# Layer 0 of a four-layer graph kernel: units sized by the spread of destinations, row sums and count copies on ScalarE, dense blocks loaded from its queue

## The reference, cut to what matters

```python
# x (6250, 256); src, dst (100000,), dst sorted and denser at low numbers; edge_weight (100000,)
edge_index = jnp.stack([src, dst])
x = _layernorm(x + L0(x, src, dst, edge_weight, L0_gnn_W), axis=-1)      # the layer that is changed
x = _layernorm(x + L1(x, edge_index, ...), axis=-1)
x = _layernorm(x + L2(x, src, dst, edge_weight, ...), axis=-1)
x = _layernorm(x + L3(x, edge_index, ...), axis=-1)

def L0(x, edge_row, edge_col, edge_val, W):
    msgs = edge_val[:, None] * x[edge_col]
    agg = jax.ops.segment_sum(msgs, edge_row, num_segments=6250)
    return agg @ W.T
```

## Time and profile before

| | |
|---|---|
| time before, median of 3 runs | 4154.18 us (4149.27 to 4157.17) |
| the profiled execution's own time | 4150.73 us |
| its span | 4149.5 us |
| granted TensorE clock, mean | 0.869 |
| DVE busy over the span | 2069.3 us (50%) |
| ACT busy | 1087.8 us (26%) |
| PE busy | 3049.1 us (73%) |
| POOL busy | 2525.4 us (61%) |
| comparison of group 0 (line 995) starts at | 69.7 us |
| last indirect transfer of layer 0's pass starts at | 1491.4 us |

### The profile page before, as it was taken

How to read it: one execution, slowest core, us unless ns; L and a number is a source line. 1 busy time by engine, 2 the same in 40 slices (tenths; PEclk the granted TensorE clock), 3 DMA queues, 4 the chain that set the end, 5 groups by cost and what they waited for, 6 DMA issues and landing times.

```text
span 4149.5 us, 56706 instructions
## 1 busy us (share of the span) xinstructions
PE 3049.1 (73%) x17920; PEld 2113.4 (51%) x17920; DVE 2069.3 (50%) x7275; ACT 1087.8 (26%) x2612; POOL 2525.4 (61%) x2372
## 2 busy tenths in 40 slices
PE   3887777777767637779957996777667675798975
PEld 2665555455555525534434554565555543555543
DVE  7998788886666526432233224432322345222249
ACT  1344444454545525500040002400000035000016
POOL 3767666665555444267736771177777744777755
PEclk9999898998989868789967998888888887899985
DMA  6666666777666647478825673554444334877743
GB/s 242 80 120 92 126 129 127 141 144 144 141 140 136 155 87 222 148 193 240 235 82 155 196 200 84 165 158 135 138 135 136 114 104 168 274 217 220 215 123 107
DMA packets 485739, 639.73 MB, mean 154 GB/s; under 512 B 79146, under 2 KB 427524, under 8 KB 480708
## 3 DMA queue, kind: packets, MB, share of 16 engines
q0 software_dynamic: 153600, 258.41, 30.6%
q1 hardware_dynamic: 331844, 377.70, 28.9%
HBM read 427.79 MB, written 208.12 MB: 153 GB/s over the span
## 4 chain that ended last, share of the span: by engine, by line
PE 24%; POOL 24%; DVE 20%; issue 14%; DMA 10%; ACT 4%; DVEq 2%; SPq 1%; POOLq 0%; ACTq 0%
POOL rows_buf L723 23%; PE PSA L754 6%; DVE accT L1169 5%; PE PSA L528 4%; DMA T<-S 3%; PE PSA L772 3%; DMA accT<-Awd 3%; DVE rows_buf L1003 2%; PE PSA L1137 2%; DMA rows_buf<-T,idx 2%; PE PSA L1038 2%; DVE accT L1177 2%; PE PSA L1219 2%; DVE big L1123 2%; DVE stat L536 1%
## 5 line engine op out<-in xcount | busy, mean ns | idle before, releaser
L1292 POOL DMA_INDIRECT A<-rows_buf,big x572 | 896.2, 1567 | 532.1 <-ACT rows_buf L1064 252.7
L723 POOL DMA_INDIRECT rows_buf<-T,idx x888 | 841.3, 947 | 293.7 <-issue 273.3
L772 PE MATMUL PSA<-S,rows_buf 128*128 128x128 bf16 (+2 forms) x5904 | 593.0, 262 | 359.7 <-DMA rows_buf<-X,idx 204.0
L772 PEld LDWEIGHTS PSA<-S,rows_buf 128*128 128x128 bf16 (+2 forms) x5904 | 553.0, 151 | 436.4 <-issue 343.7
L823 DVE TENSOR_TENSOR accT<-PSA,accT 128x256 f32 (+2 forms) x354 | 132.8, 375 | 1212.9 <-PE PSA L772 1204.2
L723 POOL DMA_INDIRECT rows_buf<-X,idx x528 | 502.4, 952 | 312.0 <-issue 309.5
L1169 DVE TENSOR_TENSOR accT<-PSA,accT 128x784 f32 (+1 forms) x444 | 360.1, 811 | 229.0 <-PE PSA L1137 160.1
L1137 PE MATMUL PSA<-big 128*128 128x272 bf16 (+2 forms) x796 | 229.4, 362 | 231.5 <-DVE accT L1169 230.3
L1054 PE MATMUL PSA<-XRS,rows_buf 128*128 128x256 f32 x1144 | 312.5, 397 | 2.1 <-ACT rows_buf L1064 2.1
L1137 PEld LDWEIGHTS PSA<-big 128*128 128x128 bf16 x796 | 76.5, 121 | 336.8 <-DVE accT L1169 320.1
L754 PE MATMUL PSA<-XRS,rows_buf 128*64 128x512 bf16 (+3 forms) x912 | 242.9, 380 | 0.0
(11 more groups left out here) (273 smaller groups left out, 5650.0 us busy)
## 6 DMA issues: line engine op xcount, KB each, us to landing
XRS<-Ad SPq DMA_DIRECT2D x144, 512.0 KB
Ad<-accT SPq DMA_DIRECT2D x28, 1568.0 KB, 6.7
rows_buf<-Ad SPq DMA_DIRECT2D x72, 512.0 KB
XRS<-in_xpad SPq DMA_DIRECT2D x192, 128.0 KB, 3.9
rows_buf<-A SPq DMA_DIRECT2D x48, 512.0 KB, 4.5
A<-accT SPq DMA_DIRECT2D x3, 6272.0 KB
Awd<-accT SPq DMA_DIRECT2D x6, 3136.0 KB, 9.9
X<-rows_buf SPq DMA_DIRECT2D x144, 128.0 KB, 1.9
```

The lines of the kernel that those rows point to most:

```text
L723: s_hg[i % RING].on(pool.indirect_dma_start(Gv(i % RING, j), None, table, bass.IndirectOffsetOnAxis(idx[:, c:c + 1], 0)), 16)
L772: last = pe.matmul(PS[i % 2][0:F, W * h:W * h + W], Gv(i % RING, j)[:, o:o + F], hits[:, i % SRING, j, :], start=j + part == 0, stop=j == ...
L1292: pool.indirect_dma_start(A, bass.IndirectOffsetOnAxis(tgt[:, c:c + 1], 0), G[:, i % RING, j, :], None, compute_op=ALU.add).then_inc(s_k[n ...
```

## The change

1. **Unit sizes.** Seven classes (CLASSES) replace four: chunks 0 to 63 in fours with 8 slots, 64 to 119 in pairs with 8, 120 to 159 in pairs with 10, 160 to 251 single with 8, 252 to 375 in pairs with 20, 376 to 447 single with 14, the rest single with 16. Units go from 444 to 366, hot ones from 192 to 156; those of windows 6 to 11 from 84 to 52, those of windows 12 to 27 from 168 to 158. The one-hot ring OHRING goes from 8 to 6, and the planner's cost is another one.
2. **Duplicates.** PE adds a third product in source_rows: 16384 is added wherever the other edge comes later, so that Eq holds only equal and not later ones. For groups below BYACT (92) the row sums of Eq are then taken by ACT (row_sums, four ACTIVATEs), DVE waits for them and compares with 1. From group 92 on DVE sums as before. targets stands at another place in DVE's order: for groups up to 92 behind the first unit_out of its own group.
3. **Late counts.** In the windows behind the hot ones (12 to 27), every second unit (83 in all: 9 of 980 columns, 36 of 686, 38 of 784) is copied from PSUM to SBUF as bf16 by ACT (unit_copy); PE's next unit waits for that copy, and DVE adds from the copy.
4. **Dense blocks.** SP issues only the loads of blocks 0 and 1; block t + 2 is issued on ACT's queue behind dense_turned(t).
5. **Waits.** In onehots, waits on units that DVE has itself added already are left out; others are for one unit later than before.

```diff
+MAXN = 20
+UC = NT * MAXN
-OHRING = 8
+OHRING = 6
...
+CLASSES = ((0, 64, 4, 8), (64, 120, 2, 8), (120, 160, 2, 10), (160, HOTW, 1, 8),
+           (HOTW, 376, 2, MAXN), (376, 448, 1, 14), (448, HOT, 1, 16))
...
+    u.copied = TURN[u.w] > LASTHOT and u.at % 2 == 1
...
-    cost = lambda u: 1.2 * u.k + 0.4
+    cost = lambda u: 1.2 + 0.7 * u.k if u.hot else 0.2 + 0.051 * u.n + u.k * (0.35 + 0.0128 * u.n)
...
-            for t in range(NT):
-                if dense_step(t) + 1 == p:
-                    dense_load(t)
+                for t in range(2):
+                    dense_load(sp, t)
...
-                pe.matmul(o, srch[:, c:c + 1].broadcast_to([128, 128]), identb[:, :], start=True, stop=False)
+                pe.matmul(o, lowerb[:, :], identb[:, :], start=True, stop=False)
+                pe.matmul(o, srch[:, c:c + 1].broadcast_to([128, 128]), identb[:, :], start=False, stop=False)
...
+        def row_sums(i):
+
+            if i < BYACT:
+                sc.wait_ge(s_eq, i + 1)
+                for j in range(CG):
+                    last = sc.activation(junkA[:, j, :], Eq[:, i % 2, j, :], ACT.Identity, accum_out=cnt[:, G0 + i, j:j + 1])
+                last.then_inc(s_rs, 1)
+
         def targets(i):
...
+            if i < BYACT:
+                v.wait_ge(s_rs, i + 1)
+                least = 1.0
...
+        def built(q):
+
+            if q.at >= spread.evicted:
+                v.wait_ge(s_am, q.at + 1)
+                if q.hot:
+                    v.wait_ge(s_amw, q.hots + 1)
...
+                before = UNITS[u.at - 1]
+                if before.copied:
+                    s_ca.of(pe, ("unit", before.at))
+                else:
+                    pe.wait_ge(s_ae, u.at)
...
+                s_ca.mark(("unit", u.at), sc.activation(ABW[:, 0:NT * u.n], AB[:, 0:NT * u.n], ACT.Identity))
...
+            if u.copied:
+                s_ca.of(v, ("unit", u.at))
+                got = ABW[:, 0:NT * u.n]
...
                     dense_turn(t)
                     dense_turned(t)
+                    if t + 2 < NT:
+                        dense_load(sc, t + 2)
+            if i + 1 < NCOLD:
+                row_sums(i + 1)
```

More of the change, by code:

```diff
@@ L78, in natural_units @@
     us = []
[L79 removed]
+    for lo, hi, k, n in CLASSES:
         for c in range(lo, hi, k):
@@ L98 @@
 TURN = {w: i for i, w in enumerate(ORDER)}
+for u in UNITS:
+    u.copied = TURN[u.w] > LASTHOT and u.at % 2 == 1
+for u in UNITS:
+    u.copies = sum(q.copied for q in UNITS[:u.at])
 def unit_at(p):
@@ L355, in build @@
     pool.tensor_copy(identb[:, :], ident[:, :])
+    pool.tensor_scalar(lowerb[:, :], lower[:, :], float(FAR), None, ALU.mult)
     pool.memset(ones[:, :], 1.0)
@@ L411, in build @@
     u = 0
-    for lo, hi, k, n in ((0, PAIR, 2, NS), (PAIR, HOTW, 1, NS), (HOTW, TWO, 2, US), (TWO, HOT, 1, US)):
+    for lo, hi, k, n in CLASSES:
         m = (hi - lo) // k
@@ L996, in equals @@
                             srcf[:, g, :].unsqueeze(2).broadcast_to([128, CG, 128]), ALU.is_equal).then_inc(s_eq, 1)
+        def row_sums(i):
[4 more added lines that the diff above has]
+                last.then_inc(s_rs, 1)
         def targets(i):
             g = G0 + i
[L1001 to L1008, removed]
+            if i < BYACT:
+                v.wait_ge(s_rs, i + 1)
+                least = 1.0
+            else:
+                v.wait_ge(s_eq, i + 1)
+                for j in range(CG):
+                    last = v.tensor_tensor_reduce(out=junk[:, j, :], in0=Eq[:, i % 2, j, :], in1=lower[:, :], scale=1.0, scalar=0.0,
+                                                  op0=ALU.mult, op1=ALU.add, accum_out=cnt[:, g, j:j + 1])
+                last.then_inc(s_cn, 1)
+                v.wait_ge(s_cn, i + i - BYACT + 1)
+                least = 0.0
+            v.scalar_tensor_tensor(cnt[:, g, :], cnt[:, g, :], least, spare[:, g, :], ALU.is_gt, ALU.mult).then_inc(s_cn, 1)
+            v.wait_ge(s_cn, i + 1 + max(0, i - BYACT + 1))
             v.tensor_tensor(tgt[:, CG * g:CG * g + CG], cnt[:, g, :], srcA[:, g, :], ALU.add).then_inc(s_b, 1)
@@ L1109, in onehots @@
                     if u.hot:
-                        before = unit_at(p - CG - 1) if n >= 2 else None
-                        if before is not None:
-                            v.wait_ge(s_amw, before.hots + before.hot)
                         v.wait_ge(s_oq, n + 1)
@@ L1117, in onehots @@
                 if p >= OHRING:
-                    before = unit_at(p - OHRING)
-                    v.wait_ge(s_am, before.at + 1)
-                    if before.hots + before.hot:
-                        v.wait_ge(s_amw, before.hots + before.hot)
+                    built(unit_at(p - OHRING))
                 width = NT * u.n
@@ L1145, in build_unit, with unit_copy @@
                     for part in range(3):
-                        last = pe.matmul(PS[7][:, 0:NC8], ohw[p // CG % 2][part][:, :, p % CG], ohk[:, p % OHRING, 0:NC8],
+                        last = pe.matmul(PS[7][:, 0:width], ohw[p // CG % 2][part][:, :, p % CG], ohk[:, p % OHRING, 0:width],
                                          start=i + part == 0, stop=i == u.k - 1 and part == 2)
                 last.then_inc(s_amw, 1)
+        def unit_copy(u):
+            if u.copied:
+                sc.wait_ge(s_am, u.at + 1)
+                for q in UNITS[:u.at]:
+                    if q.copied and q.copies == u.copies - 1:
+                        sc.wait_ge(s_ae, q.at + 1)
+                s_ca.mark(("unit", u.at), sc.activation(ABW[:, 0:NT * u.n], AB[:, 0:NT * u.n], ACT.Identity))
         def unit_out(u):
@@ L1166, in unit_out @@
                 v.wait_ge(s_azw, HWIN)
-            v.wait_ge(s_am, u.at + 1)
+            if u.copied:
+                s_ca.of(v, ("unit", u.at))
+                got = ABW[:, 0:NT * u.n]
+            else:
+                v.wait_ge(s_am, u.at + 1)
+                got = AB[:, 0:NT * u.n]
             aw = slots(Aw[buffer_of(u.w)])
-            v.tensor_tensor(aw, AB[:, 0:NT * u.n].rearrange("p (b s) -> p b s", s=u.n), aw, ALU.add).then_inc(s_ae, 1)
+            v.tensor_tensor(aw, got.rearrange("p (b s) -> p b s", s=u.n), aw, ALU.add).then_inc(s_ae, 1)
+            spread.evicted = u.at + 1
             if u.hot:
@@ L1176, in unit_out @@
                 aw = slots(Aww)
-                v.tensor_tensor(aw, PS[7][:, 0:NC8].rearrange("p (b s) -> p b s", s=u.n), aw, ALU.add).then_inc(s_aew, 1)
+                v.tensor_tensor(aw, PS[7][:, 0:NT * u.n].rearrange("p (b s) -> p b s", s=u.n), aw, ALU.add).then_inc(s_aew, 1)
         def window_clear(w, i):
@@ L1295, in spread @@
             pool.wait_ge(s_k[k], 16 * uses[k])
+        spread.evicted = 0
         equals(0)
-        targets(0)
         hot_hits(0)
```

44 lines of the change are left out of this document (26 added, 18 removed).

## The result

| | before | changed |
|---|---|---|
| median of 4 runs | 4151.73 us | 4053.08 us (4040.85 to 4059.8) |
| ratio, 95% interval | | 0.9759 (0.9731 to 0.9787) |
| profiled execution's own time | 4150.73 us | 4040.85 us |
| span | 4149.5 us | 4039.6 us |
| DVE busy | 2069.3 us | 1900.6 us |

The kernel is 98.7 us faster where 160 were forecast: right in sign and inside the range, but six tenths of the size. The profiled execution lies at the low end of the changed kernel's runs (109.9 us under that of before), so I split its difference by parts and keep the medians for the verdicts.

What follows compares the result with a forecast made beforehand. Part A was taken as bound by DVE with POOL close behind, part B by PE's waits for late dense loads, no engine full. 4150.7 + 3.5 - 52 - 94 - 15 = 3993, predicted 3990; range 3900 to 4085.

Steps and rivals of the forecast that it cites:

- Setup: Before the first group: class loops over seven classes add 19 small DVE instructions, +3.5 us, all on the path.
- Part A, DVE's sum: Groups 0 to 91: DVE's busy time falls by 128 us, from 714.5 to about 587.
- POOL late next: Groups 0 to 91: POOL limits next, 681 us of scatters plus 75.2 of transfer waits, 756; with allowance 780, -52.
- the allowance for stalls: Groups 0 to 91: 20 to 25 us added to POOL's 756 for ACT's clears and other coupling, giving 780.
- Part A, ACT's row sums: Groups 0 to 91: four row sums a group on ACT, 1.7 us a group, 156 in all, beside other work.
- The rival in which they end in series: Part A: ACT's 1.7 us a group cannot hide, +28 instead of -52, 4073 us; chance 0.09.
- Part B, the loads: Groups 92 to 142: dense loads issued earlier on ACT's queue remove PE's 94.4 us of waits, -94.
- The rival of slow loads: Loads held up by other transfers: earlier issue gains only the issue's own time, 20 us; 4067 us, chance 0.06.
- Part B, the copies: Groups 92 to 142: ACT's copies shorten PE's waits for adds; -15 us for copies and sizes, between +40 and -40.
- the two middle rivals: Row sums in series in part A (4073 us, 0.09) and loads slow, not late (4067 us, 0.06); together 0.15.
- ACT becomes the bound: Row sums in series, and in part B copies and clears hold PE: part B +55, 4237 us, chance 0.05.
- the stalls go with DVE's load: Stalls absorbed: part A 720 us, part B 421 + 10; 3886 us, half way 3940; 0.18 for under 3945.

Runs made afterwards that it cites:

- undoing one relief of DVE: Two runs on the changed kernel: triangle sums on DVE in all groups, target's old place, 4070.53 us; the four old unit classes, 4051.51 us.
- the reads moved: Changed kernel with DVE's slot offsets of windows 11 to 27 read into registers in mid window, not at the window's first unit: 3999.67 us.
- the old late class: Changed kernel without copies, slot offsets read in mid window, chunks from 376 on single with 16 slots: 3980.2 us.
- both orders mended: Changed kernel with copies, the copy of a group's second unit ahead of weigh on ACT, and slot offsets read in mid window: 3974.78 us.

## Why the prediction was right or wrong

**Setup** was +3.5 and is +3.7 us.

**Part A, DVE's sum: right.** 587 us forecast, 587.4 measured. **POOL late next: not shown.** Part A takes 751.4 us, which is the 756 of POOL's sum without the 20 to 25 that I had added for the clears; POOL's waits for ACT fell from 108.3 us to 38.5, and its waits for its own transfers stayed (75.9 for 75.2):

```profile
POOL A L1341 <- issue: 93.1, 284, 3.6
POOL A L1341 <- DMA A<-rows_buf,big: 75.9, 38, 8.6
POOL A L1341 <- ACT rows_buf L1084: 38.5, 20, 21.4
```

But if POOL alone had held part A, undoing one relief of DVE would have cost it little. By the profiled executions they cost 22.5 and 30.5 us apart (the first with the target's place) and 54.5 together. The number came near the floor, and the reasoning from the floor is not confirmed. The term mis-sized is the allowance for stalls, -52 for -84.4.

**Part A, ACT's row sums: right.** They are 298 ns with a 191 ns read each, and DVE waited for them 10.8 us in all, 17 times:

```profile
L1009 ACT ACTIVATE XRS<-rows_buf x368: 292/298/314, 74.4 to 823.8; 128x128 f32<-128x128 f32 x184
...
  DVE big L1026: 10.8, 17
```

The rival in which they end in series did not come true. ACT's busy time in part A rose by 105 us where 156 were taken. What I had too high is the gain: relieving DVE of 87 us, with the target's new place, gave 22.5 in part A, and DVE's gaps grew as its work shrank (164 us of gaps for 117.5).

**Part B, the loads: right, and confirmed apart.** -94 forecast, -86 measured in part B of the kernel with this edit alone, -81 in the medians. The rival of slow loads falls, by that run and by the one that kept SP's queue.

**Part B, the copies: wrong, and this is the step that failed.** The prediction put "-15 for copies and sizes, between +40 and -40". Measured it is +70 for the copies alone, and about nothing for the sizes (503.8 us of part B without copies against 499.8), outside both bounds. The durations were right: 0.82, 0.74 and 0.985 us for 784, 686 and 980 columns, where 0.85, 0.76 and 1.04 were taken, and DVE's add from a copy takes 0.66 and 0.58 us busy:

```profile
L1182 ACT ACTIVATE XRS<-PSA 128x784 bf16<-128x784 f32 x38 | 31.1, 819 | 31.2 <-PE PSA L1162 30.9
L1182 ACT ACTIVATE XRS<-PSA 128x686 bf16<-128x686 f32 x36 | 26.5, 736 | 19.7 <-PE PSA L1162 19.7
...
L1208 DVE TENSOR_TENSOR accT<-XRS,accT 128x784 bf16 x38 | 25.2, 663 | 62.8 <-ACT XRS L1182 62.6
```

What failed is the price of a place in an order. I had weighed 0.85 us of a copy against 0.97 of an add, and named only a clear as what might stand ahead. Weigh stands ahead of the copy of a group's second unit, with its 1.3 us, and that alone was 28 us. And I had no row, and no thought, for a register read at a window's start: in part B of the kernel before such a read took 1.92 us at most, in the changed kernel up to 7.56, and that cost 53 us beside the copies and some 4 without them. I take it that the copies had joined DVE, ACT and PE in one chain which could no longer catch up; what speaks for it is POOL's waits for ACT (113.7 us with both, 49.6 with the reads moved, 40.7 without the copies); which stretch of slack it was is not shown.

**The sum.** Had the copies cost nothing, the terms would have been 3.7 - 84.4 - 86 = -167, and the kernel without copies is at 3982.58 against 3990 forecast for the changed one. The forecast hit a kernel that the change is not. That the time still fell inside the range is luck in part: part A gained 32 us more than its term and part B 84 less than its terms, two errors of opposite sign. And 4053 lies just above the forecast's own band, 3945 to 4050, near the two middle rivals (4067 and 4073), though the mechanism of neither was there.

**The rivals.** That ACT becomes the bound was given 0.05 and the time 4237. Its mechanism, a copy that holds PE behind ACT's other work, was there, at 44.5 us of waits of PE instead of 149. That the stalls go with DVE's load did not come true either: part A stayed at 751 us where that rival had 720, and part B, even without the copies, at 504 where it had 431.

## What to carry to other kernels

Price a step that is moved to another engine by what stands ahead of it in that engine's order at the moment when it is wanted, for each of its places, before pricing its duration. When an order on a queue holds a load behind a wait, first try to swap the two on the same queue: here that gave 71 of 81 us, with no work on another engine. And look at register reads of an engine right behind a large store: in the rows of busy time and of waits they are only idle time that nothing ends, while the view of their line gives their durations. Check where their first value lies, too: a new unit size can move it.

## What the runs showed of the hardware that was not expected

The reads of slot offsets into DVE's registers in part B, in the kernel before, the changed one, and the changed one with the old unit classes:

```profile
L1154 DVEq TENSOR_LOAD <-big x26: 343/663/1915, 910.1 to 1405.2; - x26
L1188 DVEq TENSOR_LOAD <-big x24: 823/3322/7564, 830.5 to 1296.6; - x24
L1187 DVEq TENSOR_LOAD <-big x26: 343/599/1934, 867.8 to 1306.8; - x26
```

The same number of values takes several times as long in the second. What differs is where a read begins in the table of offsets: its first index is the unit's number, and with the old classes every window of part B begins at a multiple of four (values of 4 bytes), with the new ones none does from window 13 on. Over the whole pass of the ten kernels that read at a window's first unit and after each eight, reads of eight values took:

| first value | begun 0.9 to 1.6 us after a window's store | begun over 8 us after one |
|---|---|---|
| at a multiple of four | 1.75 to 1.94 us (25 reads) | 0.59 to 1.85 us, median 0.60 (250) |
| elsewhere | 7.17 to 7.77 us (15 reads) | 1.85 to 5.68 us, median 3.35 (76) |

So a read's length goes with both, the place of its first value and the nearness of a store. No run moved the offsets to multiples of four with the new classes kept, so what that would be worth is not shown, nor by what mechanism a read is held up.

The kernel before had such gaps too, at another line: a read of line 1077, begun 2.5 us after a window's store, took 6.34 us, and DVE stood idle behind it:

```profile
L1077 DVEq TENSOR_LOAD <-base x1: 6341/6341/6341, 982.5 to 982.5; - x1
989.14 0.29 DVE L1085 TENSOR_TENSOR big<-PSA,big 128x128 f32 x1 [5.65 <-issue]
```

A dense load issued on ACT's queue takes 0.366 us there, and 0.435 on SP's. In ACT's timeline no gap beside its own instructions can be seen for it.

Four kernels lie some 70 us and more under the changed one: without copies (3982.58 us), the same with the reads in mid window (3978.52) and with the old late class besides (3980.2), and the one with copies and both orders mended (3974.78). They don't differ by more than their intervals, and the first is a single line.
